# Attention 0 to attention 3 with mixtures of experts on one core: two steps of the last batch moved ahead, two tables cleared by another engine, idle products in later passages

## The reference, cut to what matters

```python
for l in range(4):
    x = x + xattn_l(layernorm(x), ctx)   # four different attentions over the context
    x = x + ffn_l(layernorm(x))          # four different mixtures of 8 experts
```

```python
top_vals, top_idx = top_k(x @ Wg + bg, 2); w = softmax(top_vals)
rank = cumsum(one_hot(top_idx))          # over all tokens, batch after batch
y = W2[e].T @ act(W1[e].T @ x)           # only for the tokens of expert e
```

## Time and profile before

| | |
|---|---|
| median of 3 executions | 1202.76 us (1201.64 to 1203.77) |
| the profiled execution, whole | 1204.15 us |
| its span, first to last instruction | 1202.4 us |
| mean granted TensorE clock | 0.912 of full speed |
| TensorE busy | 1024.1 us, 85% of the span |
| VectorE busy | 729.6 us, 61% |
| ScalarE busy | 641.0 us, 53% |
| GpSimd busy | 573.5 us, 48% |

### The profile page before, as it was taken

One profiled execution on the slowest core, in us unless ns is written; L12 is line 12 of the kernel. 1 busy time (PEld: TensorE's weight loads), 2 busy tenths in 40 slices (PEclk: granted clock), 3 DMA queues, 4 the chain that ended last, 5 costly groups with the idle time before them and its releaser, 6 DMA issues.

```text
span 1202.4 us, 21878 instructions
## 1 busy us (share of the span) xinstructions
PE 1024.1 (85%) x6653; PEld 790.4 (66%) x6653; DVE 729.6 (61%) x2451; ACT 641.0 (53%) x2115; POOL 573.5 (48%) x923
## 2 busy tenths in 40 slices
PE   4986999858899988968999997697599999976993
PEld 3864888735556567855677765686467777655993
DVE  5575344576766684277767777523876767754443
ACT  2215333336777834428887875233487888831231
POOL 5232566542000023548565666657475555664452
PEclk9986999967999987989999999698799999975997
DMA  2003456696910113220000000275200000014666
GB/s 64 13 19 99 149 166 194 213 139 232 388 37 2 36 45 116 65 68 19 1 19 2 19 2 25 69 221 146 73 19 2 2 1 2 2 41 124 190 209 189
DMA packets 116003, 102.83 MB, mean 86 GB/s; under 512 B 18027, under 2 KB 97571, under 8 KB 115888
## 3 DMA queue, kind: packets, MB, share of 16 engines
q1 hardware_dynamic: 104992, 82.45, 23.5%
q0 software_dynamic: 8448, 17.20, 4.3%
q10 hardware_dynamic: 2448, 1.80, 0.7%
HBM read 65.04 MB, written 36.36 MB: 84 GB/s over the span
## 4 chain that ended last, share of the span: by engine, by line
PE 57%; DVE 16%; POOL 8%; issue 6%; DMA 6%; ACT 5%; SPq 1%; DVEq 0%; POOLq 0%; ACTq 0%
PE ps L2695 4%; PE ps L2877 4%; PE ps L2697 4%; PE ps L2696 4%; PE ps L2891 4%; PE ps L2775 3%; PE ps L2788 3%; PE ps L3065 3%; DMA xr<-xr_d,src_i 2%; POOL yq_d L902 2%; PE ps L2905 2%; POOL xq_d L883 2%; ACT ex L1278 2%; PE ps L3416 2%; PE ps L3221 2%
## 5 line engine op out<-in xcount | busy, mean ns | idle before, releaser
L1278 ACT ACTIVATE ex<-ps,nmx 128x154 f32<-128x154 f32 x512 | 193.9, 391 | 70.2 <-DVE nmx L2199 68.7
L1065 POOL TENSOR_TENSOR pp<-ex,rc 128x256 f32<-128x256 f32 x256 | 157.6, 615 | 145.5 <-DVE rc L2204 144.7
L2199 DVE TENSOR_REDUCE nmx<-ps 128x2 f32<-128x308 f32 x256 | 119.4, 469 | 61.7 <-PE ps L2697 61.3
L2877 PEld LDWEIGHTS ps<-ident,pp 128*128 128x128 f32 x640 | 73.8, 142 | 57.5 <-POOL pp L1066 49.3
L2695 PE MATMUL ps<-kp,q_s 128*128 128x308 f32 x256 | 96.4, 377 | 14.9 <-ACT ex L1278 7.7
L902 POOL DMA_INDIRECT yq_d<-yq,ids_q x78 | 74.7, 957 | 71.6 <-DVE yq L1961 52.9
L1278 ACT ACTIVATION_READ_ACCUMULATOR ex<-ps,nmx 128x1 f32 x512 | 105.1, 205 | 0.0
L2877 PE MATMUL ps<-ident,pp 128*128 128x128 f32 x640 | 100.0, 280 | 4.8 <-POOL pp L1066 4.8
L1402 ACT ACTIVATE pe<-ps,nmx 128x154 f32<-128x154 f32 x256 | 84.4, 395 | 29.4 <-DVE nmx L2080 28.4
L872 POOL TENSOR_TENSOR ln_r<-ln_v,mhalf 128x4 f32<-128x4 f32 x32 | 34.7, 1084 | 95.7 <-DVE ln_v L1696 77.6
L2696 PE MATMUL ps<-kp,q_s 128*128 128x308 f32 x256 | 79.8, 312 | 0.0
(11 more groups left out here) (448 smaller groups left out, 2756.0 us busy)
## 6 DMA issues: line engine op xcount, KB each, us to landing
w_r<-in_L_ffn_W SPq DMA_DIRECT2D x69, 256.0 KB, 3.4
xq_d<-blankq SPq DMA_DIRECT2D x4, 4160.0 KB, 23.9
w_q<-in_L_ffn_W SPq DMA_DIRECT2D x46, 256.0 KB
w_q<-in_L_ffn_w SPq DMA_DIRECT2D x46, 128.0 KB
xq<-xq_d SPq DMA_DIRECT2D x22, 130.0 KB, 2.5
w_s<-in_L_ffn_W SPq DMA_DIRECT2D x8, 256.0 KB
w_e<-in_L_ffn_W SPq DMA_DIRECT2D x8, 256.0 KB, 5.1
acc<-yq_d SPq DMA_DIRECT2D x8, 256.0 KB, 4.5
```

The costliest lines, as they stand in the source:

```text
L1065: pool.tensor_tensor(pp[st % 2][:, m % 4, 2 * j:2 * j + 2, :], w[:, :, 0:P], r.broadcast_to([P, 2, P]), ALU.mult)
L1278: ins = act.activation(ex[:, tt % NEX, j, :], ps[:, tt % 3, j * SK:(j + 1) * SK], ACT.Exp, bias=nmx8[:, tt % 8, j:j + 1], accum_out=sm8[:, ...
L2199: dve.tensor_reduce(nmx8[:, tt % 8, :], ps[:, tt % 3, 0:2 * SK].rearrange("p (h s) -> p h s", h=2), AX.X, ALU.max, negate=True).then_inc(n ...
L2877: last = pe.transpose(ps[:, bank, k * P:(k + 1) * P], pp[st % 2][:, k, c, :], ident[:, :])
```

## The change

One. VectorE's `choose` is cut into `largest` (logits, two largest) and `experts_of` (indices and marks). For batches 0 and 1 the two follow each other as before. At the end the order becomes `largest(2)`, `scale(1, 3)`, `experts_of(2)`, `largest(3)`, `experts_of(3)`, `ranks(2)`, `runs_of_experts()`. TensorE runs `xT_of(1, 3)` and `choices(3)` ahead of `rank(2)`. ROUTE_V and ROUTE_P follow.

Two. The two fills of kz1 leave GpSimd. ScalarE writes the zeros instead (the number one times zero, by two ACTIVATE instructions of 128 x 2464) after `tanh(1)` and ahead of `xT_of(1, 2)`; VectorE's first `prep1` waits for them with a new semaphore.

Three. Idle products: other numbers in the choice of layer 0, and new ones at the end of attention 1 (22), at the starts of attentions 2 and 3 (12 and 8 each, the first with a wait for the seventh expert's output, whose bank they write), and ahead of the experts of layers 2 (16) and 3 (2).

```diff
         ROUTE_V = ("gr", 0), ("d", 0), ("oh", 0), ("kr", 0), ("place", 0), ("gr", 1), ("d", 1), ("oh", 1), ("kr", 1), ("place", 1), ("gr", 2), ("d", 2), \
-            ("oh", 2), ("kr", 2), ("place", 2), ("gr", 3), ("d", 3), ("oh", 3), ("expert", 0), ("expert", 1), ("kr", 3), ("place", 3), ("what", 0), ("what", 1), \
+            ("oh", 2), ("gr", 3), ("d", 3), ("oh", 3), ("kr", 2), ("place", 2), ("expert", 0), ("expert", 1), ("kr", 3), ("place", 3), ("what", 0), ("what", 1), \
...
-        ROUTE_P = ("lg", 0), ("rank", 0), ("lg", 1), ("rank", 1), ("lg", 2), ("rank", 2), ("lg", 3), ("count", 0), ("rank", 3), ("bias", 0), ("list", 0), \
+        ROUTE_P = ("lg", 0), ("rank", 0), ("lg", 1), ("rank", 1), ("lg", 2), ("lg", 3), ("rank", 2), ("count", 0), ("rank", 3), ("bias", 0), ("list", 0), \
@@ GpSimd, before_heads
-                        pool.memset(kz1[u][:, :, :].bitcast(F32), 0.0)
                         pool.memset(pr1[u][:, :, :, SK - P:], 0.0)
                         pool.memset(vv1[u][:, :, :, :], 1.0)
                         ins = pool.memset(vr1[u][:, :, :], 1.0)
@@ ScalarE, sorted_runs
                 tanh(1)
+                for u in range(2):
+                    act.activation(kz1[u][:, :, :], ones[:, 0:1].rearrange("p (a c) -> p a c", a=1).broadcast_to([P, 4, B * SK]), ACT.Identity, scale=0.0).then_inc(n_kz, 1)
                 xT_of(1, 2)
@@ VectorE, prep1
                             dve.wait_ge(n_zero, min(l, 2))
+                            if l == 1:
+                                dve.wait_ge(n_kz, 2)
@@ VectorE, sorted_runs
-                choose(2)
+                largest(2)
                 scale(1, 3, x_tok)
+                experts_of(2)
+                largest(3)
+                experts_of(3)
                 ranks(2)
-                choose(3)
                 runs_of_experts()
@@ TensorE, region
+                idle_products(2, 16 if l == 2 else 2)
                 columns(0)
@@ TensorE, heads
                     prep(l, 1, i)
+                if l == 2:
+                    pe.wait_ge(k_y, E - 1)
+                idle_products(5, 12)
                 turned_x(0)
+                idle_products(5, 8)
@@ TensorE, heads1
                 logits1(1)
+                idle_products(5, 5)
                 tail_xT(l, 2)
                 out(NST - 1)
                 logits1(2)
                 turned_out(3)
+                idle_products(5, 3)
                 project(3)
                 rank(1)
+                idle_products(5, 3)
                 rank(2)
+                idle_products(5, 3)
                 tail_xT(l, 3)
+                idle_products(5, 3)
                 logits1(3)
                 prep(2, 0, 0)
+                idle_products(5, 5)
                 rank(3)
@@ TensorE, sorted_runs
                 choices(2)
-                idle_products(0, 12)
-                rank(2)
+                idle_products(0, 7)
                 xT_of(1, 3)
                 choices(3)
-                idle_products(0, 8)
+                rank(2)
+                idle_products(0, 4)
                 count()
                 rank(3)
+                idle_products(0, 10)
                 biases()
+                idle_products(0, 8)
                 lists()
```

More of the change, by code:

```diff
@@ L486, in xattn_moe_stack @@
         c_hi_ok = sem("c_hi_ok"); c_ok = sem("c_ok")
-        n_raw = [sem("n_raw0"), sem("n_raw1")]; n_wk0 = sem("n_wk0"); n_wo1 = sem("n_wo1"); n_wo = sem("n_wo"); n_zero = sem("n_zero")
+        n_raw = [sem("n_raw0"), sem("n_raw1")]; n_wk0 = sem("n_wk0"); n_wo1 = sem("n_wo1"); n_wo = sem("n_wo"); n_zero = sem("n_zero"); n_kz = sem("n_kz")
         n_x = sem("n_x"); n_xl = sem("n_xl")
@@ L2426, in begin, with largest @@
                     statistics(1, b, x_tok)
-                def choose(b):
+                def largest(b):
                     rows = tiles(b)
@@ L2438, in choose, with experts_of @@
                     dve.tensor_tensor(r_d[:, rows].rearrange("p (n a) -> p n a", a=1), m8[:, rows, 1:2], m8[:, rows, 0:1], ALU.subtract).then_inc(s_v, 1)
+                def experts_of(b):
+                    rows = tiles(b)
                     for n in range(b * TB, (b + 1) * TB):
@@ L2578, in sorted_runs @@
                 begin(1)
-                choose(0)
+                largest(0)
+                experts_of(0)
                 context_weights(2)
@@ L2586, in sorted_runs @@
                 begin(2)
-                choose(1)
+                largest(1)
+                experts_of(1)
                 scale(1, 2, x_tok)
```

## The result

Nine executions of the changed kernel took 1190.5 to 1199.4 us, median 1194.4; nine of the kernel before, beside them, 1201.6 to 1207.0, median 1204.1. The ratio is 0.992 [0.990, 0.994]: about 9.7 us or 0.8% faster. The forecast was 9.4 us. The profiled execution of the changed kernel took 1192.93 us with a span of 1190.7 us, 11.7 less than before, at a mean granted clock of 0.930 (0.912 before).

What follows compares the result with a forecast made beforehand. Bound taken: passages between attentions, with TensorE at lower clock, VectorE stalled by GpSimd's fills, and GpSimd's sends. 5.0 + 2.6 + 1.7 + 0.1 = 9.4 us off 1202.76 gave 1193.4; 8 in 10 between 1189.5 and 1199.

Steps and rivals of the forecast that it cites:

- A: Choice of layer 0, from batch 2's second-largest difference to `runs_of_experts`: 5.0 us gained, 3.7 at half clock.
- the 3.3 us of stalls: Choice of layer 0: two VectorE rows blocked under GpSimd's large fills, 1.73 + 1.57 us, counted within A's gain.
- B: End of attention 1: idle products keep the clock up, 2.6 us gained; bounds -3.3 and +4.
- first leg: B, scaling of batch 2 to sum of batch 3: the sum was to come about 1.8 us earlier.
- second leg: B, sum of batch 3 to its logits: transposes and logits at full clock, no separate size given.
- third leg: B, logits of batch 3 to its target rows: the second hole in GpSimd's sends goes, 0.7 us.
- The fourth: B's leg from target rows to layer 1's first output rows: TensorE's some 6 us lead mostly turns into waiting.
- D: Start of layer 2's experts: 16 idle products, first scatter 1.7 us earlier; bounds -3.4 and +1.7.
- C: Starts of attentions 2 and 3, and layer 3's experts: 0.1 us gained, between -0.3 and +0.8.
- rival 2: Start of layer 0's experts or the load after the sends gains too: 2 to 4 us more, some 1190; chance 0.17.
- Rivals 1 and 3: 1: clock falls anyway, only A stays, some 1198.4, chance 0.16; 3: cold idle products delay due work, 1207.0, 0.05.
- rival 4: Choice of layer 0: small fills or ScalarE's clears still stall VectorE, A shrinks by 3.3 us, 1196.7; chance 0.10.

Runs made afterwards that it cites:

- e9: The kernel before, unchanged, profiled a second time, on a slower chip; 1245.0 us.
- e4: The changed kernel without the 22 idle products at the end of attention 1; 1197.4 us, ratio 0.993 to the kernel before.
- e3: The changed kernel without any new idle product after the choice of layer 0; ratio 0.993 to the kernel before, 6.6 us faster.
- e5: The changed kernel with 10 more idle products at the end of attention 1, ahead of layer 1's experts; 1198.2 us, ratio 0.994 to the kernel before.
- e7: The changed kernel without 9 of the 22 idle products at the end of attention 1; ratio 0.993 to the kernel before.
- e8: The changed kernel itself, unchanged, run once more; 1194.0 us, ratio 0.991 to the kernel before.
- e6: The changed kernel with GpSimd's remaining eight small fills moved after its first gathers; ratio 0.992 to the kernel before.
- e12: The same kernel as e11, run on a chip like the first; 1194.3 us, ratio 0.989 to the kernel before.
- e10: The changed kernel with the edits of both e5 and e6, on the slower chip; ratio 0.999 to the kernel before, 2.4 us faster.
- e1: The kernel before with only the two fills of kz1 moved from GpSimd to ScalarE; 1198.4 us, ratio 0.994.
- the bridge: The 10 idle products that e5 adds to the changed kernel, ahead of the transposes that start layer 1's experts; e5 measured 1198.2 us.
- e2: The changed kernel's choice of layer 0, with kz1 fills still on GpSimd and no new idle products in later passages; ratio 0.999 to the kernel before.
- third group: The runs e9, e10 and e11, on a slower chip where the kernel before took 1245.0 us; times compared only within the group.
- e11: e10 without the 12 and 8 idle products at the starts of attentions 2 and 3, on the slower chip; ratio 0.997 to the kernel before, 5.7 us faster.

## Why the prediction was right, and where it was not

The time was right to 1 us, and it was so partly by luck: terms that came smaller were made up by stretches that the forecast had not in its sum. In the two profiles the sum 5.0 + 2.6 + 1.7 + 0.1 became 5.05 - 0.18 + 1.30 + 0.77, which is 6.9; the other 4.8 us of the 11.7 lie elsewhere.

**A** was forecast as 5.0 us and came as 5.05 in the profile after. Its pieces: a stall by the small fills of 0.5 (forecast 0.4), transposes to logits 2.50 (2.44), logits to `runs_of_experts` 3.77 (3.87). The split between clears and order was about right too: 4.2 and 1.8 us alone (3.3 and 1.7). What the prediction lacked is the spread. It took the 3.3 us of stalls for a fixed price; e9 shows 6.1 us for one instruction. And the upper bound of 1.57 us for the small fills was passed by e4, 1.9 us (3.02 less 1.11). The six profiles with the changed kernel's choice (after, e3, e4, e5, e7, e8) have 8.39 to 10.66 us, a mean of 9.3, so A is worth 4.1 us on average against the first profile of before, and 7.9 against the second. The small fills do hold VectorE up, by 0.5 us in five profiles and 1.9 in one, and in e6, where they are gone, it is 0. The Trainium skill, "SBUF — State Buffer", section "SBUF: two separate sides", which the prediction named as speaking against this change, was right there; the trace agrees, with 1.61 and 3.02 us under the fills against 1.11. The ScalarE clears fell between their bounds, at 2.2 us. The estimate that the prediction took from the Trainium skill, "ScalarE: Activation LUTs", section "Rules for kernel authors", was 2.35.

**B** is the step that failed: "Gain at the last send 1.8 + 0.7 = 2.5", and with it "I take 2.6". The first leg gained 1.0 us in the profile after and 1.4 as a mean of five. The clock did not stay up, as the step had assumed; in after and e8 it fell 1.6 and 1.7 us ahead of the sum of batch 3, in the other three (e5, e6, e12) 3.7 to 3.8 us behind it. What makes it fall early or late is open: e10, with the edits of e5 and e6, has it early again. Where the fall came early, idle products at the lower clock delayed the transposes (second leg +0.9; in e7, without these products, +0.0). The third leg gained its 0.7. The fourth, priced as mere waiting, lost 1.0 against the first profile (0.6 against the mean of before and e1 to e4, which have no idle products at the end of attention 1): the wait of 2.30 us for the load was itself what lowered the clock for the products behind it. That was shown by e5 and e12, where the leg is 19.05. Within the passage B gave 0.7 us without the bridge (41.2 as the mean of after, e8 and e6, against 41.9 of the five profiles without tail products) and 3.4 with it, of which the bridge has 1.3 to 1.5 and the late fall of the clock the rest.

The passage alone misleads, though. With the next one added, up to the first maxima of attention 2, the eight profiles with tail products (13 of the 22 in e7) need 98.2 to 99.4 us, with the bridge or without. The six without need 98.3 and 98.5 us (e1, before) or 102.0 to 103.0 (e2, e3, e4, e9). The means are 98.7 and 101.0, so up to there the tail products may be worth about 2.3 us after all, near the 2.6 of the forecast but not at the place and not by the way it gave; the bridge shows no gain there. Whether the tail products keep that later stretch at full clock, or its clock fell so by chance, no run separates.

**D** was 1.7, and measures 1.3 in the profile after, 1.4 between the means of the table's first eleven rows. Behind the first transposes the path to the first scatter got 1.9 us shorter (6.82 to 4.95), but the 16 products hold these transposes up by some 0.5 us, which the prediction put at 0.3 and held for hidden. What it lacked is that the gap of 3.61 us it fills isn't there on every chip: on the slower one D cost 3.2 us.

**C** was 0.1. The profile after is 0.77 us shorter between the maxima of attention 2 and layer 2, which e8, the same program, isn't; from the last moments ahead of attention 3 (849.30 before) to the maximum at 892.25 e1, without C, has the short length (42.15 us) and e8, with it, the long one (43.09). In the third group the kernel without C even has the lower median, 1239.3 against 1242.6, with intervals that overlap. No gain, as forecast.

**Not in the forecast but in the time**: three stretches. The first is the start of layer 0's experts at full clock, 1.75 us (part of rival 2); of the ten profiles with the new order and the clears on ScalarE two, e3 and e8, have a fall of the clock there and need 20.1 and 20.3 us, so that the mean gain is 1.2. The second is 1.49 us ahead of A, where a stretch at the lower clock that the first profile has at 76.52 was absent. The same program has such a stretch again in e8 (77.70 to 81.11), so it is chance. The third is 1.56 us from layer 2's first output rows to a maximum in attention 3: the seven profiles on chips like the first that have D need 102.0 to 103.8 us there, the four without 103.9 to 105.5, which hints at D's work but has no cause shown. Rivals 1 and 3 did not come in full, though a piece of each did at the end of attention 1; rival 4 came in e4's execution, for 1.9 us.

## What to carry to other kernels

A fill on one engine that blocks another is not a fixed price: look how many follow back to back, for the blocked engine may get its turn only after the last, and move the small ones too. Idle products stand in front of work, so what they are worth hangs on the gap they fill: the same 16 gained 1.3 us in a gap of 3.6 us and cost 3.2 where the gap was 0.5. When a stage gets ready earlier, look for the new wait behind it; and add the next passage before you count the gain, for the bridge's 1.3 us were gone 60 us later. Before a gain of a few us is credited to an edit from two profiles, measure the same program twice: here that alone was 8.9 us, so judge passage by passage over several kernels that share the passage.

## What the runs showed of the hardware

- VectorE's conversion stood 6.28 us under ten GpSimd fills (e9), and a scaling 3.02 us until the last of eight small ones ended (e4); in other executions of the same instructions VectorE got in between, at 1.90 and 1.61 us. What decides it is open.
- Stretches at the lower clock fall at other moments in each execution, and two passages have their length by it. The start of layer 0's experts takes 17.5 to 17.6 us, 19.2 or 19.3 with a stretch of 3.4 us within (before, e9) and 20.1 or 20.3 with one of 6.8 us (e3, e8). From layer 1's outputs to attention 2 it is 56.95 us on chips like the first (57.5 and 58.0 in e10 and e11), 58.5 with a stretch of 3.4 us that begins 20 us ahead of the end (e6), and 60.1 to 60.2 with one of 6.8 us that begins 24 us ahead of it (e2 to e5, e9, e12).
- From layer 0's first result rows to the end of attention 1 the profiles on chips like the first need 302.7 to 309.9 us, whatever the edit; the two of the changed kernel itself, after and e8, 307.65 and 307.40.
- One chip needed 1245.0 us for the kernel that takes 1204 to 1206 on the others, 37 of the 43 us between e9's profile and the first arising between the attentions: 10.6 from layer 0's first result rows to the heads of attention 1, 18.6 from the end of attention 2 to the heads of attention 3, and 8.0 from the end of attention 3 on. Within attentions 2 and 3 the distance of the two profiles stays the same within 0.1 us.
